# Moving evacuations, row halves and copies within the issue order of two attention layers

## The reference

```python
# layer 0: 16 heads of 32
qn, kn, vn = layer_norm(x), layer_norm(ctx), layer_norm(ctx)
Q, K, V = qn @ wq + bq, kn @ wk + bk, vn @ wv + bv
attn = softmax(Q K^T / sqrt(32)) per head
x = x + (attn V) @ wo + bo
x = x + gelu(layer_norm(x) @ w1 + b1) @ w2 + b2
# layer 1: 16 heads of 64
Q, K, V = x @ Wq, ctx @ Wk, ctx @ Wv
attn = softmax(Q K^T / sqrt(64) - 2.0) per head
out = layer_norm((attn V) @ Wfc + x) * gamma + beta
```

## Time and profile before

| | |
|---|---|
| median of 3 runs | 1438.63 us |
| profiled execution | 1436.97 us, span 1435.2 us |
| PE busy | 1369.2 us, 95% |
| DVE, ACT, POOL busy | 885.3, 685.3, 438.7 us |
| layer 0, steps with projections | about 100 to 466 us, some 51 us a unit |
| layer 0, last two steps | about 466 to 511 us |
| MLP and queries of layer 1 | about 512 to 702 us |
| layer 1 | about 702 us to the end, 43 us a unit |

### The profile page before, as it was taken

How to read it: one execution, slowest core, us unless ns; L and a number is a source line. 1 busy time by engine, 2 the same in 40 slices (tenths; PEclk the granted TensorE clock), 3 DMA queues, 4 the chain that set the end, 5 groups by cost and what they waited for, 6 DMA issues and landing times.

```text
span 1435.2 us, 31553 instructions
## 1 busy us (share of the span) xinstructions
PE 1369.2 (95%) x12865; PEld 876.1 (61%) x12865; DVE 885.3 (62%) x1583; ACT 685.3 (48%) x1322; POOL 438.7 (31%) x488
## 2 busy tenths in 40 slices
PE   6999999999998789999999999999999999999997
PEld 4556666666665555544556666666666666666665
DVE  6778888978876868444345545455545445545565
ACT  3557766667745745221234444434444434444432
POOL 3125666666665721200001211111211111211123
PEclk9999999999999889999999999999999999999999
DMA  8226444445352054133432333322242412333421
GB/s 264 68 65 175 128 126 100 123 124 155 88 158 76 17 193 147 38 117 115 112 72 53 101 72 105 72 82 54 59 113 63 113 41 54 100 73 92 101 69 40
DMA packets 117533, 140.56 MB, mean 98 GB/s; under 512 B 49789, under 2 KB 91789, under 8 KB 115341
## 3 DMA queue, kind: packets, MB, share of 16 engines
q1 hardware_dynamic: 116201, 136.28, 35.1%
q10 hardware_dynamic: 1188, 2.27, 0.5%
HBM read 63.15 MB, written 21.35 MB: 59 GB/s over the span
## 4 chain that ended last, share of the span: by engine, by line
PE 48%; DVE 3%; issue 1%; ACT 1%; POOL 0%; POOLq 0%; ACTq 0%; DVEq 0%
PE attn_p_proj L985 17%; PE attn_p_proj L980 14%; PE attn_p_max L1008 3%; PE attn_p_sc L1225 2%; PE attn_p_sc L1039 2%; PE attn_p_sc L1038 2%; PE attn_p_pv L1067 1%; PE attn_p_proj L1147 1%; PE attn_p_pv L1066 1%; PE attn_p_pv L1068 1%; DVE attn_nmax L1609 1%; PE attn_p_max L1147 1%; DVE attn_knat L1642 1%; ACT attn_probs L1373 1%; ACT attn_knat L1402 0%
## 5 line engine op out<-in xcount | busy, mean ns | idle before, releaser
L1609 DVE TENSOR_REDUCE attn_nmax<-attn_p_max 100x1 f32<-100x722 f32 x250 | 225.8, 903 | 114.8 <-PE attn_p_max L1008 112.1
L691 POOL TENSOR_TENSOR attn_probs<-kernel_w_first,attn_probs 128x400 f16<-128x400 f32 x96 | 90.6, 943 | 671.5 <-ACT attn_probs L1373 671.5
L985 PE MATMUL attn_p_proj<-kv_w_v,attn_ctxT 128*128 128x512 f16 (+1 forms) x1152 | 264.3, 379 | 0.0
L1363 ACT ACTIVATE kernel_w_first<-attn_p_sc,attn_score_bias 128x400 f32<-128x400 f32 x192 | 113.5, 591 | 307.9 <-PE attn_p_sc L1039 307.9
L980 PE MATMUL attn_p_proj<-attn_ctxT,kv_w_k 128*128 128x361 f16 x1536 | 249.1, 317 | 4.1 <-DVE attn_knat L1642 3.5
L691 POOL TENSOR_TENSOR attn_probs<-attn_p,attn_probs 128x400 f16<-128x400 f32 x182 | 191.6, 1057 | 152.8 <-ACT attn_probs L1373 147.2
L980 PEld LDWEIGHTS attn_p_proj<-attn_ctxT,kv_w_k 128*128 128x128 f16 x1536 | 144.6, 97 | 88.6 <-DVE attn_knat L1642 9.7
L985 PEld LDWEIGHTS attn_p_proj<-kv_w_v,attn_ctxT 128*128 128x128 f16 (+1 forms) x1152 | 110.4, 101 | 111.0
L1363 ACT ACTIVATE attn_p<-attn_p_sc 128x400 f32<-128x400 f32 x192 | 96.2, 501 | 133.9 <-PE attn_p_sc L1035 129.6
L985 PE MATMUL attn_p_proj<-l_w_v,attn_ctxT 128*128 128x512 f16 (+1 forms) x576 | 132.2, 379 | 1.5 <-DVE attn_vbuf L1648 1.4
L980 PE MATMUL attn_p_proj<-attn_ctxT,kernel_w_first 128*128 128x361 f16 x768 | 128.0, 317 | 0.0
(11 more groups left out here) (284 smaller groups left out, 2599.1 us busy)
## 6 DMA issues: line engine op xcount, KB each, us to landing
kv_w<-attn_knat SPq DMA_DIRECT2D x128, 180.5 KB, 3.4
attn_kstack<-attn_knat SPq DMA_DIRECT2D x192, 90.2 KB, 2.2
ctx_turned<-attn_ctxT SPq DMA_DIRECT2D x8, 1444.0 KB, 8.4
attn_ctxT<-ctx_turned SPq DMA_DIRECT2D x8, 1444.0 KB, 8.4
attn_kstack_b<-attn_knat SPq DMA_DIRECT2D x64, 180.5 KB, 3.6
attn_c<-in_ctx_dram SPq DMA_DIRECT2D x35, 256.0 KB, 3.1
kv_w_v<-in_L_xattn_w_dram SPq DMA_DIRECT2D x7, 1024.0 KB, 5.8
q_parts<-attn_probs SPq DMA_DIRECT2D x16, 200.0 KB, 2.5
```

The source lines that it names most:

```text
L691: eng.tensor_tensor(probs[:r, g % 2, 1, t, :HG * SQ], p32[:r, t % 3, :], probs[:r, g % 2, 0, t, :HG * SQ], ALU.subtract).then_inc(p_lo_mad ...
L985: last = pe.matmul(bank[:r, :], ctxT[:, cpar, ca, k, P * t:P * t + r], w_v[:, wa, k, c0:c0 + E], **flags)
L1363: act.activation(p32[:r, t % 3, :], p_sc[:r, t % 2, :HG * SQ], ACT.Exp, bias=bias_col[:r, 0:1] if score_bias else 0.0).then_inc(exp_made, 1)
L1609: dve.tensor_reduce(nmax[:SQ, hh:hh + 1], max_banks(u, g, hh)[:SQ, :, :HALF], AX.XY, ALU.max, negate=True).then_inc(max_made, 1)
```

## The change

It reorders instructions within the engines' own queues. No arithmetic is added or removed. In words, by layer and engine:

- Layer 1, PE: in slot 10 of the steps 1 to 15 the transpose of the maxima stands behind the projection of that slot, and not ahead of the value products.
- Layer 1, ACT: in slots 1, 2 and 3 the first evacuation stands ahead of the exponential.
- Layer 0, DVE: the low half of the last value tile (a = 13) of the units 1 to 6 moves from slot 22 to slot 0 of the next step, behind the first maximum.
- Layer 0, POOL: `out_lo` moves from slot 12 to the front of slot 11.
- Layer 0, step U-1, ACT and DVE: in slots 16 and 22 the evacuation, in slots 10, 16 and 22 `row_hi`, and in slots 14 and 20 `row_copy` stand at the front of the slot; `row_lo` moves one slot ahead, to the front of the slot of `row_hi`.
- Layer 0, step U: `copy_pv` of group 2 moves from slot 23 to slot 21, behind `row_final` of tile 4, and `normalise` of group 1 from the front of slot 18 to slot 21.

```diff
@@ -398,2 +398,3 @@
         self.row_place = [4, 9, 13, 17, 18]
+        self.evac_first = (16, 22)
         self.row_acc, self.row_sum, self.row_stat, self.row_pow, self.row_centre = 0, 2, 3, 4, 5
@@ -1179,3 +1180,4 @@
                         scores(s, s - 1, 1 - par, g, t)
-                    if layer == 1 and s > 0:
+                    turn_behind = layer == 1 and (s == 0 or j == KT * (NG - 1) + MAX_T)
+                    if layer == 1 and not turn_behind:
                         turns(s, kind, j)
@@ -1196,3 +1198,3 @@
                             project(s, par, cpar, a)
-                    if layer == 1 and s == 0:
+                    if turn_behind:
                         turns(s, kind, j)
@@ -1449,2 +1451,9 @@
                     g, t = divmod(j, KT)
+                    early = sl.evac[j][:1] if proj and (layer == 1 and 1 <= j < KT - 2 or layer == 0 and s == U - 1 and j in sl.evac_first) else []
+                    for a in early:
+                        evacuate(s, par, a)
+                    if layer == 0 and s == U - 1 and sl.row_tile(s, j, sl.row_hi) is not None:
+                        row_hi(sl.row_tile(s, j, sl.row_hi))
+                    if layer == 0 and s == U - 1 and sl.row_tile(s, j, sl.row_copy) is not None:
+                        row_copy(sl.row_tile(s, j, sl.row_copy))
                     if has_scores:
@@ -1476,8 +1485,8 @@
                         act.activation(next_weights[i][1][:, k], next_w32[i][:, k], ACT.Identity, scale=WS).then_inc(next_hi_made, 1)
-                    if sl.row_tile(s, j, sl.row_copy) is not None:
+                    if s != U - 1 and sl.row_tile(s, j, sl.row_copy) is not None:
                         row_copy(sl.row_tile(s, j, sl.row_copy))
-                    if sl.row_tile(s, j, sl.row_hi) is not None:
+                    if s != U - 1 and sl.row_tile(s, j, sl.row_hi) is not None:
                         row_hi(sl.row_tile(s, j, sl.row_hi))
                     if proj:
-                        for a in sl.evac[j]:
+                        for a in sl.evac[j][len(early):]:
                             evacuate(s, par, a)
@@ -1778,2 +1787,7 @@
                         nxt = (s, 0) if proj else None
+                    early = sl.evac[j][:1] if layer == 0 and s == U - 1 and j in sl.evac_first else []
+                    for a in early:
+                        evacuate(s, par, a)
+                    if layer == 0 and s == U - 1 and sl.row_tile(s, j, sl.row_hi) is not None:
+                        row_lo(sl.row_tile(s, j, sl.row_hi))
                     if nxt and t < HG:
@@ -1786,2 +1800,4 @@
                             split_max(s, *nxt, prev)
+                    if layer == 0 and j == 0 and 1 < s < U:
+                        evacuate(s - 1, 1 - par, NPROJ - 1)
                     if layer == 0 and prep:
@@ -1822,3 +1838,3 @@
                             copy_pv(s - 2, NG - 1)
-                        if g > 0 and has_scores:
+                        if g > 0 and has_scores and (layer, s, g) != (0, U, NG - 1):
                             copy_pv(s - 1, g - 1)
@@ -1834,4 +1850,5 @@
                     if proj:
-                        for a in sl.evac[j]:
-                            evacuate(s, par, a)
+                        for a in sl.evac[j][len(early):]:
+                            if layer == 1 or a < NPROJ - 1 or s == U - 1:
+                                evacuate(s, par, a)
                     if layer == 0 and s == U and j == sl.last_bias_t:
@@ -1842,3 +1859,5 @@
                         row_final(sl.row_tile(s, j, sl.row_final))
-                    if sl.row_tile(s, j, sl.row_lo) is not None:
+                        if (s, sl.row_tile(s, j, sl.row_final)) == (U, EARLY - 1):
+                            copy_pv(s - 1, NG - 2)
+                    if sl.row_tile(s, j, sl.row_lo) is not None and s != U - 1:
                         row_lo(sl.row_tile(s, j, sl.row_lo))
@@ -2058,2 +2077,4 @@
                     g, t = divmod(j, KT)
+                    if layer == 0 and outs and j == sl.out_lo_t - 1 and s != U + 1:
+                        out_lo(s)
                     if has_scores and j > 0 and (layer == 0 or (t - 1) % 2 == 0) and (s - 1, *divmod(j - 1, KT)) not in sl.shared_lo:
@@ -2067,3 +2088,3 @@
                             normalise(s - 1, g - 2)
-                    if layer == 0 and s == U and j == KT * (NG - 1):
+                    if layer == 0 and s == U and j == KT * (NG - 1) + MAX_T - 1:
                         normalise(s - 1, 1)
@@ -2074,3 +2095,3 @@
                             normalise(s - 1, g - 1)
-                    if outs and j == sl.out_lo_t and not (layer == 0 and s == U + 1):
+                    if layer == 1 and outs and j == sl.out_lo_t:
                         out_lo(s)
```

## The result

The kernel after takes 1413.62 us, the median of four runs (1411.65 to 1414.63), beside 1438.5 for the kernel before on the same chip (1437.93 to 1440.14). The ratio is 0.9824, with a 95% interval of 0.9807 to 0.9841. The forecast was 1413.6. Its profiled execution took 1414.61 us, span 1412.8, which is 22.4 less than the profiled execution of before; the medians lie 25 apart, since the one profile of before was a short run and the one of after a long one.

What follows compares the result with a forecast made beforehand. PE, busy 95% of the span, was taken as the bound, leaving 66.0 us idle to win. Terms summed to 26.3 us, less 1.3 held back: 25.0 off the 1438.63 median, 1413.6 us, range 1407 to 1424.

Steps and rivals of the forecast that it cites:

- Layer 1, 12.9 predicted: Layer 1: 7.0 us from 14 transpose waits, 5.9 from key projection waits, one of 17 (step 1, slot 2) left out.
- The price of a wait: PE's waits: each costs its idle time plus 0.17 us, by which a matmul is shown longer than its step.
- The third rival: Layer 1: the late transpose holds DVE's queue at `place_max`, up to 2.75 us a unit lost, 1460 us; 4%.
- Tile 13: 3.1: Layer 0, slot 1: six waits for the first maximum's reduction go when the evacuation moves behind it, 3.1 us.
- `out_lo`: 2.6: Layer 0, slot 15: five waits shrink as DVE's context half no longer stands still beside POOL; 2.6 us, bounds 0 and 3.9.
- The rest of 0.25 a wait: Layer 0, slot 15: estimated 0.25 us left of each of five waits, as the reduction needs the preceding maximum.
- my upper bound of 3.9: Layer 0, slot 15: most that moving `out_lo` could win, five waits at 0.77, 3.85 us.
- Step U-1, 3.0 predicted: Layer 0, step U-1: 1.4 us at the output's transpose (waiting for `row_copy`) and 1.6 at the value projection.
- The turn, 2.3 predicted: Layer 0, slots 22 and 23 before step U: 1.0 us at an exponential's wait, 1.3 at row tile 3's sum.
- Step U, 0.9 + 1.5 predicted: Layer 0, step U: 0.9 us from `out_lo`, 1.5 from `normalise` and `copy_pv`; the latter bounded by 4.25 gain, 1.64 loss.
- The first rival: End of layer 0: a knot where PE's gains are waited for one slot on; 18.6 us less, 1420.0 us; 18%.
- The second rival: Step U: with fewer waits PE keeps 2.4 GHz; 4 of 6.7 us come, 1409.6 us; 10%.

Runs made afterwards that it cites:

- e1: Kernel before with one edit: layer 1's maxima transpose in slot 10 of steps 1 to 15 behind the projection; 0.9949, 1431.82 us.
- e2: Kernel before with one edit: in layer 1's slots 1, 2 and 3 ACT does the first evacuation ahead of the exponential; 0.9953, 1431.68 us.
- e3: Kernel before with one layer 0 edit: the last value tile's low half on DVE moved from slot 22 to the next step's slot 0; 0.9974, 1434.86 us.
- e4: Kernel before with one layer 0 edit: POOL's `out_lo` at the front of slot 11, not in slot 12; 0.9992, 1438.34 us.
- a1: Kernel after with `out_lo` back in slot 12 in step U-1 only; 0.9802, 1411.64 us.
- a4: Kernel after with step U-1's edits on ACT and DVE undone (evacuations of slots 16 and 22, `row_hi`, `row_copy`, `row_lo`); 0.9882, 1421.74 us.
- a7: a1 with DVE's low half of the MLP weights moved from slot 22 to slot 7 of step U; 0.9802, 1410.59 us.
- a2: Kernel after with `out_lo` back in slot 12 in step U only; 0.9818, 1413.08 us.
- a5: Kernel after with step U's moves of both `normalise` of group 1 and `copy_pv` of group 2 undone; 0.9819, 1412.96 us.
- a6: Kernel after with `normalise` of group 1 back at the front of slot 18, `copy_pv` left in slot 21; 0.9815, 1412.77 us.
- a3: Kernel after with `out_lo` back in slot 12 in both steps U-1 and U; 0.9806, 1410.57 us.

## Why the prediction was right, and where it was not

**Layer 1, 12.9 predicted, 12.91 measured.** Both terms hold singly: 7.0 against 6.94 (e1), 5.9 against 5.96 (e2). The price of a wait, idle time plus 0.17, holds: 14 waits of 4.6 us in all gave 6.94. The one wait left out is the one that stands. The third rival named a real thing, DVE idle at the placed maxima, but the slack behind it was enough.

**Layer 0, steps 2 to 7.** Tile 13: 3.1 against 3.3 (e3). `out_lo`: 2.6 against 3.91 (e4), 4.2 with slot 18 of step 6, which lies behind A. The rest of 0.25 a wait that I let stand is there (0.10 idle, 0.27 with the 0.17). At slot 15 the gain is 2.9, since one of the five waits was 0.95 and not 0.60. Missing in the prediction was the second wait of the same chain: the late reduction also delayed `place_max`, and slot 18's first scores waited for it, 0.16 to 0.28 a step. That my upper bound of 3.9 was met is chance. The unit step fell from about 50.9 to 49.5, 1.4 and not 1.1.

The Trainium skill's page "SBUF — State Buffer" (the two sides of the SBUF) has the shared port pair held for the whole instruction. As the prediction read it, with the pair DVE's at that instruction's end, it would have made this 0; e4's M-A says 3.91. Every stretched row here ends behind a POOL operation. In three of them DVE's end lies 0.55 behind the end of the second POOL operation: 332.55 and 332.00, 431.51 and 430.96 in the kernel after, 433.33 and 432.78 in e4. The rule's reading is the commoner case all the same. Of the larger DVE operations with two inputs that the trace of the kernel before shows stretched by over 0.3 us, the five context halves of slot 13 were held over two POOL operations. The 17 others were held over the first alone, and 16 of them ended 0.43 or 0.55 behind it.

**Step U-1, 3.0 predicted.** The edits on ACT and DVE are worth 3.5 on their own (a1 against e3), 2.95 of it at the two waits that were priced. The step of the prediction that failed is the one on `out_lo`: I priced its move by the five waits that it removes, in the steps that have them. But it is moved in step U-1 too, where there was no wait to remove, and there it puts two POOL operations onto another operation of DVE. I had a bound for that (0 for the term, "if another POOL operation falls on the context half"), but it spoke of the context half alone. It costs 1.5 in the kernel after (a1), and 4.85 where the other edits are missing (e4, some 1.7 of it clock). In A-B the kernel after won 1.02; 2.67 without its half clock.

**The turn, 2.3 predicted, 2.45 measured (B-C).** Some 0.46 of it is the clock's; against a4, whose order here is that of before, it is 1.99. The two waits that were priced gave 1.13 and 1.11, for 1.0 and 1.3. The waits left are 1.20 + 0.55 + 1.44, of which I had foreseen the first. The chain on DVE from the row sum to the split of the maxima sets this stretch, as a7 shows: what is taken out at its front is waited for at its end.

**Step U, 0.9 + 1.5 predicted, 1.17 measured (C-D).** By parts, `out_lo` gives 0.6 up to slot 16, `copy_pv` 1.4 and `normalise` 0.5 from slot 22 on, and 1.3 is lost between them to a half clock (6.30 against 5.01). So the terms hold in their stretches; the medians of a2, a5 and a6 show none of them. The first rival (what PE wins is waited for again one slot on) is right for a part of this step. The wait of 2.11 shows it best. DVE has there a reduction, a copy, a low half, the last reduction and the split in a row, 3.7 us in the kernel after (479.72 to 483.42) and 3.4 before (490.15 to 493.59). The split's last operation, on 100x4 elements, was stretched beside POOL (kernel after, POOL and DVE):

```profile
482.45 0.95 POOL L692 TENSOR_TENSOR attn_probs<-attn_p,attn_probs 128x400 f16<-128x400 f32 x1
```

```profile
479.72 0.90 DVE L1618 TENSOR_REDUCE attn_nmax<-attn_p_max 100x1 f32<-100x722 f32 x1
...
481.50 0.90 DVE L1618 TENSOR_REDUCE attn_nmax<-attn_p_proj 100x1 f32<-100x722 f32 x1
...
482.64 0.78 DVE L1627 SCALAR_TENSOR_TENSOR attn_nmax_parts<-attn_nmax,attn_nmax_parts 100x4 f16<-100x4 f32 x1
```

Before, PE went through the same slots at 1.2 GHz (clock 0.50, the last but two of the columns), came late, and waited only 0.35 for the same chain:

```profile
489.39:492.81 3.42, 3.30 (x44) 3.09 (x45) 3.42 (x6) 1.83 (x4) 2.43 (x5) 0.50 0.00 0
```


**The sum.** 12.91 + 6.80 + 2.67 + 1.99 + 2.46 = 26.8 without what the half clock made, against 26.3 before I held 1.3 back. That the median came out at the forecast to 0.1 us is partly luck: `out_lo` was 1.3 too low in the steady steps, its loss of 1.5 in U-1 was missing, and the 1.3 held back for new waits stood in for the clock.

**The clock** was the unknown of up to 2 either way. In this one execution it made 1.65 in A-B, 1.29 in C-D and 1.29 in D-E against the change, and 0.46 in B-C for it, 3.8 net, and none of it is shown to belong to an edit. The second rival, that PE would keep its clock through step U, did not come: PE is at half clock from 469.56, 483.21, 493.45 and 500.27 on there. The mean clock from B to D did rise, from 0.78 to 0.88, but where DVE's chain sets the time that won little.

## What to carry to other kernels

A wait with one named releaser, whose work stands in the wrong place in a steady loop, can be priced to a few per cent: idle time plus the pipeline's overlap, times the count, provided that what the moved work passes is longer than what it needs. Follow the late operation's chain further: a second wait of 0.12, too short to be printed, cost 0.28 a step here. Where a move is written as a rule over all steps, price it in each step where it applies, also in those without the wait, and list there which DVE operations now fall beside two POOL operations in a row. In a stretch where PE and DVE are equally busy, reckon with DVE's chain, not with PE's waits.

## What the runs showed of the hardware

- A DVE operation with two tensor inputs that started beside a running POOL operation was held over that one and the next: 2.19, 2.66 and 2.52 us where it takes 0.68 alone. It then ended 0.55 behind the second, although a third POOL operation was queued in the kernel after (430.92, 1.39 long where its like takes 0.94). It is not always two, and mostly one: in the earlier trace rows 1.42, ending 0.43 behind the first. In the trace of the kernel before 17 such operations were held over one and five over two. What decides was not tried.
- Executions with the same order up to there have a stretch of PE at 1.2 GHz or not (435.42 to 438.83 in the kernel after, none in a2, a5, a6). That one, on a busy PE, costs 1.65, and one of 3.1 to 3.4 us between slots 16 and 22 costs 1.3 to 1.5. While DVE's chain is what ends last, it costs little or nothing: C to slot 16 is 14.65 at a mean clock of 0.77 (before) and of 0.85 (a3).
- The start differs from run to run: M lies between 130.36 and 132.66 in the fourteen traces, with no edit ahead of it. A single pair of spans is not good to 2 us.
